# Decoder layer on one core: approximate attention scores in four row groups, banks by batch, and a new order

## What is computed

```python
def mixer(x, W_q, W_kv, W_o):
    q = (x @ W_q.T).reshape(B, S, H, hd); kv = (x @ W_kv.T).reshape(B, S, H, hd)
    qf = _l2_normalize_complex(fft(q)); kvf = _l2_normalize_complex(fft(kv))
    kvf = cumsum(kvf, axis=1)
    return ifft(qf * kvf).real.reshape(B, S, D) @ W_o.T

def cross(q, k, v):
    scores = einsum('bhqd,bhkd->bhqk', qh, kh) / sqrt(hd)
    scores = where(causal, scores, MASKED_BIAS)
    return einsum('bhqk,bhkd->bhqd', softmax(scores), vh)

def feed_forward(x, weight, rram_variation):
    x_q = ternary_quantize(x, 0.33, 0.5)
    w_q = ternary_quantize(weight, 0.2, 0.6)
    return einsum('bsd,od->bso', x_q, w_q + rram_variation)

x = _layernorm(x + mixer(x, W_q, W_kv, W_o))
x = _layernorm(x + cross(x, ctx, ctx))
x = _layernorm(x + feed_forward(x, weight, rram_variation))
```

## Time and profile before

| | us |
|---|---|
| median of 3 runs | 166.7 |
| lowest and highest | 166.58, 167.3 |
| the profiled execution, whole | 166.76 |
| its span, first to last instruction | 165.0 |
| granted TensorE clock, mean | 0.97 |

### The profile page before, as it was taken

The page is one execution under the profiler, slowest core; times in us unless marked ns, Lnnn a source line. Parts: engine busy times, 40 slices in busy tenths (PEclk is TensorE's granted clock), DMA queues, the critical chain, the costliest instruction groups (busy, mean ns, idle before and its releaser), DMA issues.

```text
span 165.0 us, 4546 instructions
## 1 busy us (share of the span) xinstructions
PE 146.9 (89%) x1612; PEld 98.6 (60%) x1629; DVE 140.1 (85%) x428; ACT 128.2 (78%) x342; POOL 95.1 (58%) x205
## 2 busy tenths in 40 slices
PE   7999999998999998999999999999899979897460
PEld 2746656567657556676776767765667647564230
DVE  0289899999999899989898989999899998868830
ACT  3466488888695986778989788878989979798642
POOL 4031550482690786156769834888477786778511
PEclk9999999999999999999999999999999999999855
DMA  3986566212033722122101554130312210101101
GB/s 107 288 270 177 175 161 216 79 52 68 0 116 106 204 63 60 35 57 76 36 0 38 162 156 99 56 105 2 90 41 43 96 28 2 36 32 36 64 34 64
DMA packets 16583, 14.56 MB, mean 88 GB/s; under 512 B 2352, under 2 KB 14512, under 8 KB 16560
## 3 DMA queue, kind: packets, MB, share of 16 engines
q1 hardware_dynamic: 16560, 14.26, 29.5%
HBM read 12.16 MB, written 2.10 MB: 86 GB/s over the span
## 4 chain that ended last, share of the span: by engine, by line
PE 47%; DVE 28%; ACT 15%; issue 4%; POOL 4%; POOLq 0%; ACTq 0%
PE p L727 8%; PE p L778 6%; PE p L747 6%; DVE x L2121 5%; ACT dev L1474 5%; PE p L762 5%; PE p L805 4%; PE p L768 3%; PE p L792 3%; ACT probs L1456 3%; PE p L785 3%; DVE ssq L2038 3%; PE p L733 2%; DVE unit L2054 2%; DVE r L2082 2%
## 5 line engine op out<-in xcount | busy, mean ns | idle before, releaser
L349 POOL TENSOR_SCALAR_AFFINE_SELECT probs<-probs 128x512 f32<-128x512 f32 x64 | 41.5, 664 | 10.1 <-ACT probs L1456 9.5
L2121 DVE TENSOR_REDUCE x<-p 128x4 f32<-128x512 f32 x64 | 41.7, 683 | 1.7 <-PE p L762 1.0
L1456 ACT ACTIVATE probs<-p 128x512 f32<-128x512 f32 x64 | 34.7, 595 | 4.7 <-PE p L778 4.5
L727 PE MATMUL p<-w_in,xT_s 128*128 128x512 f32 x64 | 30.3, 603 | 0.7 <-ACT w_in L1416 0.4
L343 POOL TENSOR_TENSOR rstd<-ve,power 128x1 f32<-128x1 f32 x48 | 26.9, 563 | 2.4
L338 POOL TENSOR_SCALAR ve<-spread 128x1 f32<-128x1 f32 x48 | 10.5, 218 | 29.6 <-ACT dev L1474 27.8
L1474 ACT ACTIVATE dev<-r,neg 128x256 f32<-128x256 f32 x48 | 24.2, 505 | 4.3 <-DVE neg L2094 4.2
L778 PE MATMUL p<-x1T,keys 32*128 32x128 f32 x512 | 18.8, 283 | 1.2 <-ACT x1T L1452 0.8
L778 PEld LDWEIGHTS p<-x1T,keys 32*128 32x128 f32 x512 | 15.8, 186 | 5.7 <-DVE x L2121 3.8
L785 PE MATMUL p<-probs,vals 128*32 128x128 f32 x512 | 18.1, 276 | 0.9 <-DVE att L2131 0.5
L762 PE MATMUL p<-keys,x1T_b 128*128 128x512 bf16 x47 | 16.4, 391 | 1.7 <-ACT probs L1456 1.1
(11 more groups left out here) (71 smaller groups left out, 282.8 us busy)
## 6 DMA issues: line engine op xcount, KB each, us to landing
vals<-ctxV SPq DMA_DIRECT2D x16, 256.0 KB, 2.9
x_s<-x SPq DMA_DIRECT2D x16, 128.0 KB, 2.7
xT_s<-xT SPq DMA_DIRECT2D x16, 128.0 KB, 2.6
keys<-ctxK SPq DMA_DIRECT2D x64, 32.0 KB, 2.2
out<-res SPq DMA_DIRECT2D x16, 128.0 KB, 1.7
wq_s<-w_q SPq DMA_DIRECT2D x1, 256.0 KB, 2.7
wkv_s<-w_kv SPq DMA_DIRECT2D x1, 256.0 KB, 3.7
woT_s<-w_oT SPq DMA_DIRECT2D x1, 256.0 KB, 3.9
```

The lines of the kernel that those rows point to most:

```text
L349: nc.gpsimd.affine_select(out=part, in_=part, compare_op=ALU.is_ge, fill=0.0, base=0, pattern=[[0, GH], [1, TOK]], channel_multiplier=-1). ...
L727: last = nc.tensor.matmul(p[PROJ[n]][:], xT_s[n % XR][:, g, :], w_in[:, g, :], start=(g == 0), stop=(g == 1))
L1456: nc.scalar.activation(probs[n % 2][:, c, :, :].rearrange("p g q -> p (g q)"), p[ROWS + c][:], ACT.Exp, scale=HD ** -0.5).then_inc(exps[c], 1)
L2121: nc.vector.tensor_reduce(x1[n % X1R][:, GH * c:GH * (c + 1), HD], p[ROWS + c][:].rearrange("p (h k) -> p h k", h=GH), AX.X, ALU.max, nega ...
```

## The change

The keys become compact: 128 partitions by four groups by 128 keys, head `4 g + s` in slot `s` of group `g`, with its 16 features, a row of ones, and a bar of 15 rows that now shares a row among nine queries (`SHARE`) by steps of 2^13. All of it is prepared in the input, so that a batch is one transfer of 256 KB, and `blank`, `barred_s` and the semaphores `keys_blank` go. There are six buffers instead of five.

`approximate` becomes 16 matmuls of 32 rows by 128 columns, four slots beside each other, each slot with its own bank, and one semaphore behind the last. `row_max` reads heads of one slot instead of one group. Approximate scores, exact scores and weighed values take banks by tables (`APPROX`, `SCORES`, `OUT`) from all eight. One of the two copies of the folded weights moves to VectorE. The lists of all engines are in a new order, and the other bank tables are new.

```diff
-KV = 5
-STEP_UP, BARRED, LEAK = 2.0 ** 43, 2.0 ** 40, 2.0 ** -3
+KV = 6
+SHARE, STEP = 9, 13
+TOP, LEAK = 60, 3
...
+OUT = (5, 2, 6, 1, 4, 2, 0, 4, 5, 1, 4, 2, 5, 1, 0, 4)
+APPROX = ((7, 1, 0, 2), (2, 6, 1, 3), (3, 1, 2, 0), (0, 7, 2, 4), (1, 7, 2, 3), (2, 3, 5, 7),
...
+SCORES = ((7, 4, 2, 0), (2, 1, 4, 7), (1, 7, 6, 4), (3, 1, 0, 2), (4, 2, 6, 1), (0, 2, 3, 1),
...
-        keys, vals = ring("keys", KV, [128, HEADS, TOK]), ring("vals", KV, [128, HEADS, SLOT])
+        keys, vals = ring("keys", KV, [128, GROUPS, TOK]), ring("vals", KV, [128, HEADS, SLOT])
...
             def load_keys(n):
-                for s in range(GH):
-                    sp.dma_start(keys[n % KV][SLOT * s:SLOT * s + HD, s::GH, :], ctxK[n, s]).then_inc(keys_in[n % KV], 16)
+                sp.dma_start(keys[n % KV][:], ctxK[n]).then_inc(keys_in[n % KV], 16)
...
-            def approximate(n, c):
+            def approximate(n):
 
-                high = keys[n % KV][:, GH * c:GH * (c + 1), :].rearrange("p h k -> p (h k)").bitcast(bf16)
-                nc.tensor.matmul(p[ROWS + c][:], x1T_b[n % 2][:, c, :], high[:, 1::2],
-                                 start=True, stop=True).then_inc(approx[c], 1)
+                high = keys[n % KV][:].rearrange("p g k -> p (g k)").bitcast(bf16)[:, 1::2]
+                for g in range(GROUPS):
+                    for s in range(GH):
+                        slot = slice(SLOT * s, SLOT * (s + 1))
+                        last = nc.tensor.matmul(p[APPROX[n][s]][:, g * TOK:(g + 1) * TOK], x1T_b[n % 2][slot, g, :],
+                                                high[slot, g * TOK:(g + 1) * TOK], start=True, stop=True)
+                last.then_inc(approx, 1)
...
-                        last = nc.tensor.matmul(p[ROWS + s][:, g * TOK:(g + 1) * TOK], keys[n % KV][slot, GH * g + s, :],
+                        last = nc.tensor.matmul(p[SCORES[n][s]][:, g * TOK:(g + 1) * TOK], keys[n % KV][slot, g, :],
...
-                nc.vector.tensor_reduce(x1[n % X1R][:, GH * c:GH * (c + 1), HD],
-                                        p[ROWS + c][:].rearrange("p (h k) -> p h k", h=GH), AX.X, ALU.max,
+                nc.vector.tensor_reduce(x1[n % X1R][:, c::GH, HD],
+                                        p[APPROX[n][c]][:].rearrange("p (h k) -> p h k", h=GH), AX.X, ALU.max,
```

More of the change, by code:

```diff
@@ new lines, in _ @@
+            square_roots(10)
+            round_x1(5)
+            act.wait_ge(scored, 4)
+            exponentials(3, 3)
+            exponentials(3, 0)
+            exponentials(3, 1)
+            exponentials(3, 2)
+            act.wait_ge(proj, 12)
+            square(11)
+            act.wait_ge(xqT, 1)
+            copy_xqT(0)
+            act.wait_ge(x1T_b_done, 6)
+            copy_x1T_b(5)
+            deviations(2, 1)
+            act.wait_ge(ssq_done, 12)
+            log_norms(11)
+            deviations(7, 0)
@@ new lines, in _ @@
+            act.wait_ge(rsA_done, 13)
+            square_roots(12)
+            square(13)
+            act.wait_ge(scored, 5)
+            exponentials(4, 0)
+            exponentials(4, 2)
+            exponentials(4, 3)
+            act.wait_ge(ssq_done, 14)
+            log_norms(13)
+            act.wait_ge(proj, 15)
+            square(14)
+            exponentials(4, 1)
+            act.wait_ge(neg_done[1], 4)
+            deviations(3, 1)
+            act.wait_ge(ssq_done, 15)
+            log_norms(14)
@@ L1849, in _ @@
             root_norms(15)
+            deviations(11, 0)
+            act.wait_ge(rsA_done, 16)
+            square_roots(15)
+            act.wait_ge(pv_done[2], 6)
+            copy_outT(5)
+            act.wait_ge(scored, 8)
+            exponentials(7, 2)
+            exponentials(7, 3)
+            exponentials(7, 0)
+            exponentials(7, 1)
+            act.wait_ge(yT, 15)
+            copy_yT(14)
+            round_x1(10)
+            copy_x1T(8)
+            act.wait_ge(xqT, 5)
@@ L1924, in _ @@
+            copy_outT(13)
+            act.wait_ge(neg_done[1], 13)
+            deviations(12, 1)
+            act.wait_ge(scored, 16)
+            exponentials(15, 0)
+            act.wait_ge(xqT, 11)
+            copy_xqT(10)
+            exponentials(15, 2)
             act.wait_ge(stored[0], 64)
             result(8)
[L1926 to L1931 removed]
```

3054 lines of the change are left out of this document (1458 added, 1596 removed).

## The result

| | us | ratio to before, 95% interval |
|---|---|---|
| before, median of 4 runs | 166.69 (166.58 to 167.3) | |
| the changed kernel, median of 4 runs | 162.35 (161.25 to 163.23) | 0.9729 (0.9665 to 0.9794) |
| the same kernel in a later comparison (e5 below) | 162.41 (162.39 to 162.91) | 0.9735 (0.9705 to 0.9765) |

The change makes the kernel 4.3 us faster, 2.7%. I had forecast faster, by 2.2 us, 1.3%. The sign is right, the time lies in the range, and the size is half of what it is.

A forecast was written before the change was run, and what follows sets the result against it. VectorE was taken to set the pace up to batch 15's last maximum, that batch's chain afterwards. Span: 165.0 - 0.55 - 0.8 - 3.9 + 3.0 = 162.75; with 1.76 around it 164.5 us, range 161.3 to 167.8.

The forecast's parts named there:

- relief and new waits cancel, 0: Ahead of the last maximum: fewer bank waits and new waits for whole calls and four banks offset; VectorE's idle time unchanged.
- the cut: End of batch 15's last row maximum, dividing the kernel into two stages; at 143.7 us before, forecast near 138.4.
- the call at 0.65: Approximate call of 16 small matmuls on TensorE: 0.65 us instead of 0.88, bounds 0.42 to 0.75, without overlap 1.08.
- The stage behind the cut, +3.0: After batch 15's last maximum: more ScalarE calls, delayed scores and a later feed-forward lengthen it 3.0 us, bounds 2.0 to 3.7.
- The moved work, -3.9: 13 more VectorE calls go behind batch 15's last maximum, so that maximum ends 3.9 us earlier.
- VectorE's busy time: Whole kernel: about 137 us, with 3.6 us of blanking less and one weight copy more.
- The blanking copy, -0.8: Head, VectorE: removing the 1.22 us copy at 10.73 us gains 0.8 us, since it mostly filled a wait.
- The head, -0.55: Head: with one weight copy on VectorE, the first projection starts near 6.95 us instead of 7.50, 0.55 us earlier.
- The rival of a deeper gain: The call costs 0.42 us, TensorE saves 7 us and VectorE's waits on it nearly all go: 161.5 us, chance 0.2.
- new waits: Rival: row maxima wait for whole calls and calls for four banks, costing 2 us: 166.5, no change, chance 0.14.
- TensorE as the bound: Rival: small matmuls overlap badly, 1.08 us a call, TensorE has 3.2 us more work: 167.7, up to 169, chance 0.17.
- an order that gives nothing by itself: Rival: the last maximum doesn't come earlier and the tail's 3.0 us stays: up to 168, part of the slower case.

The follow-up runs named there:

- e5: The changed kernel unaltered, measured and profiled again in a later comparison: 162.41 us, ratio 0.9735 to the kernel before.
- e13: Changed kernel with the 16 small matmuls of each approximate call exchanged for four wide ones (128 rows by 512 columns), one signal: 163.63 us, ratio 0.9809.
- e1: Changed kernel with the approximate call of every batch issued twice in a row: 162.97 us, ratio 0.974.
- e9: Changed kernel with the approximate call of every batch issued three times in a row: 163.75 us, ratio 0.9811.
- e16: Changed kernel with four wide matmuls a call, one signal, plus six unread 128x2048 copies, three each on VectorE and ScalarE: 167.21 us, ratio 1.0018.
- e10: New order, banks and six key buffers, but old blockwise keys, four transfers a batch, blanking copies and four wide matmuls a call: 167.69 us, ratio 1.0047.
- e15: Changed kernel with four wide matmuls a call, each chunk signalling by itself in the order VectorE takes them: 162.74 us, ratio 0.9748.
- e14: Kernel before, old order and banks, with compact keys in one transfer, no blanking copies, wide matmuls chunk by chunk: 167.05 us, ratio 1.0016.
- e3: Changed kernel with six unread VectorE reductions (3.9 us in all) added ahead of batch 15's last row maximum: 164.55 us, ratio 0.9846.
- e4: Changed kernel with six unread VectorE reductions (3.9 us in all) added behind batch 15's last row maximum: 164.57 us, ratio 0.9838.
- e7: Changed kernel with five unread 128x2048 copies at the old blanking places, three on VectorE, two on ScalarE: 162.82 us, ratio 0.9736.
- e6: Kernel before, old order and banks, with compact keys, no blanking, one transfer, and four small matmuls of one row group per chunk: 169.83 us, ratio 1.017.
- e8: Changed kernel with the call's two loops exchanged, so the four matmuls of one row group follow each other: 162.1 us, ratio 0.9704.

## Why the prediction came out as it did

**The step that failed is "relief and new waits cancel, 0".** I had held VectorE's idle time ahead of the cut constant, and had called this my most uncertain choice. It went from 8.1 to 4.7 us. The forecast had the stage ahead of the cut 4.7 us shorter (0.8 and 3.9) and the one behind it 3.0 longer. Measured, the first is 6.8 to 6.9 us shorter and the second 2.9 to 3.1 longer (the table: 133.6 to 126.8 and 126.7, 18.5 to 21.6 and 21.3). So all of the 2 us that I missed lie ahead of the cut. e13 takes the small matmuls away and has 128.8 there, 4.8 us less than before, which is the forecast: what is missing, 2.0 to 2.1 us, is what the shorter call gives. I had priced the call at 0.65, on the side of the f32 score row; it is 0.34, below my lower bound of 0.42. And I had counted a wait for the whole call that doesn't exist at this length (0.0 ahead of L2065), while it is 4.0 us at 0.90 (e13). With the call at 0.65, as the sum had it, the time would lie between e1 (0.57, 163.0) and e9 (0.80, 163.75), still about a us below the 164.5 of the sum. So it isn't the price of the call alone: at that price too relief outweighs new waits.

In pricing the call I took the 32 rows of the score call for pairs. They are single instructions, two to each of its 16 matmuls, so 34 ns is the price of one; the 0.55 for sixteen isn't changed by it. That half of that price is issue is not what the runs show for bf16: in e1 and e9 each further matmul costs 14 ns, a quarter of the 0.055 us in which 128 columns stream (a quarter of 0.22).

**The stage behind the cut, +3.0: met, but not by my reasons alone.** ScalarE took 11.9 us from the copy of x1T of batch 15 (138.31) to the deviations of its second normalisation (150.23), where it took 9.6: 2.3 longer, where I had 2.9. The rest is in part TensorE's clock, which my sum doesn't have. e13 is only 1.8 us longer than before behind the cut. The two stages, e13 and then e5 (the granted clock is the third number from the end), and their last feed-forwards:

```profile
139.22:159.45 20.23, 13.52 (x199) 9.11 (x197) 15.77 (x67) 17.29 (x47) 15.37 (x33) 1.00 0.14 48
```

```profile
136.54:157.88 21.34, 14.71 (x199) 9.86 (x197) 15.77 (x68) 17.18 (x47) 15.52 (x33) 0.92 0.13 45
```

```profile
155.33 1.68 PE L810 MATMUL p<-w_ffn,xqT_s 128*128 128x256 bf16 x12
```

```profile
152.72 2.77 PE L813 MATMUL p<-w_ffn,xqT_s 128*128 128x256 bf16 x12
```

From the cut to the last ternary transpose both take 15.99 us. Then the same twelve matmuls take 1.68 us at full clock and 2.77 at the lower, 1.1 us more, and that is the whole difference between the two stages. Before the change the last two feed-forwards also ran at the lower clock (1.46 us for six matmuls, against 0.83), with 0.81 granted behind the cut. In the profiles TensorE kept its clock to the last matmul in e13, e9 and e16, but not in the changed kernel, nor in e10 and e15, which have the wide call too (2.76 and 2.13 us). The mean clock also differs between executions of one kernel (0.976 to 0.996 in the changed kernel, the fastest of its four having 0.996), so how much of this belongs to a kernel stays open.

**The moved work, -3.9: the size right, the reason not.** VectorE has 3.84 us more behind the cut, and in e13 "ahead" fell by 4.8. But VectorE's busy time ahead of the cut fell by only 3.0 us from e14, the old order without blanking, to e13; 1.8 are less idle time (9.1 to 7.4, counted from the first sum of squares). And e3 and e4 show that such a us isn't worth 1 ahead and well under half behind. A sum by two stages isn't false, it describes; it doesn't say what a further edit would bring.

**VectorE's busy time, 139.2 where I had 137.** The blanking copies are gone, yet steps of the same form take longer in the new order. The first ternary step, before and after:

```profile
L2112 DVE TENSOR_SCALAR above<-x 128x256 bf16<-128x256 f32 x16 | 5.0, 309 | 0.1
```

```profile
L2056 DVE TENSOR_SCALAR above<-x 128x256 bf16<-128x256 f32 x16 | 6.5, 405 | 0.2
```

The scaling of the normalisations (439 to 503 and 494 ns) and the shift (188 to 278) behave alike, while steps that read a bank are as before (unit vectors 684 and 678). Ahead of the cut VectorE is 1.0 us busier than in e13, so a part of what the small matmuls free there is used up in this way. One such step of 0.60 us, at 140.59, falls on a mask of GpSimd (139.56 to 141.04); whether that is the cause wasn't tried.

**The blanking copy, -0.8: worth nothing** (e14: 152.05 against 152.02 us of body; e7). I had given the copy at 10.73 0.8 us because it filled a wait only in part. VectorE's busy time ahead of the cut is 1.1 us less in e14 and its idle time 1.1 more.

**The head, -0.55: not met, and not settled.** The warming matmuls were to end near 6.95 and free the projection, which started at 7.68 and 7.22. The folding `dft_s,wkv_s` ahead of them began at 5.96 and 5.83 where it had begun at 5.53 before (its weights took 4.1 us from issue to landing by the page of the changed kernel, 3.7 by that of before). The first sum of squares was at 10.30 and 9.84 in the two profiles, around the 10.13 of before. The means over the profiles of either order, 10.0 and 10.4, leave room for some 0.4 us. A term of half a us from one profile of a head that varies by a whole one can't be read there.

**The balance.** By medians the new order brought 3.3 us and the small matmuls 1.2. By the profiles the order alone (e13) has the stage ahead of the cut as I had forecast it and the small matmuls take 2.1 us more off it, of which 1.1 was lost again to the clock in these executions. The rival of a deeper gain named the right mechanism, the waits of the earlier trace rows going, with too high a price: it had 3.0 us for what brought 1.2 by medians. Three rivals fell: new waits (none at L2065), TensorE as the bound (it is 142.2 busy), and an order that gives nothing by itself (e13). That the time came to lie in the range is no proof of the sum: the 3.0 us behind the cut were met partly by a clock that isn't in it.

What stays open is why the new order is shorter. In e13 the bank waits of the earlier trace rows are nearly gone, and VectorE has more give in the changed kernel (e3); whether the banks by batch or the sequence of steps do it wasn't tried apart, since each order is written for its banks.

## What to carry to other kernels

A smaller matmul and an order that can use it are one change: chunk by chunk in the old order the small matmuls cost 1.7%, in the new order they gave some 0.7%, and the order gave 1.9% without them. Where two engines are both full, price an edit by adding known work in both stages before summing it: here a us of VectorE was worth 0.5 to 0.8, a us of TensorE 0.1 to 0.2, and no stage had the full price. Compare profiles without their heads where the head varies by more than the effect, and look at the granted clock of each stage before a difference of a us is explained by waits.

## What the hardware showed that I had not expected

A call of 32-row matmuls between full-width work costs 0.33 us from start to start for 4 matmuls of one row group (e6) and 0.34 for 16 in four (changed kernel), 0.57 for 32 (e1) and 0.80 for 48 (e9). Each matmul beyond the 16 thus costs 14 ns, a quarter of the 0.055 us in which 128 columns stream: the four row groups overlap in full. What is left of a call above its stream is 0.11 to 0.12 us. The Trainium skill ("TensorEngine Tiling (Array Packing)", Key Properties) says that a change of the tiling mode drains the array; this rest agrees in kind, and no run shows a drain by itself. The Trainium skill ("TensorE: Matmul & The Clock Gate", Part 3) lets weight loads overlap with running matmuls only in another row group; the order of the row groups should then matter, and in e8 it cost 0.03 us a call.

One copy of 1.91 us in the wrong queue was followed by a stand of TensorE of 2.33 us and by the lower clock for the next stretch, together up to 5 us (an estimate, see e16). And twelve matmuls at the very end took 1.68 or 2.77 us by the clock alone, in kernels whose steps there are the same.
